# Both tables made straight from x1, three of them kept in DRAM, first batches last in their slot, and e1 spread by TensorE

## What is computed

```python
def _L0_gnn_ref(V, adj, w1, w2, w3, bias):
    o1 = jnp.matmul((adj == 1).astype(jnp.float32), jnp.matmul(V, w1))
    o2 = jnp.matmul((adj == 2).astype(jnp.float32), jnp.matmul(V, w2))
    o3 = jnp.matmul((adj == 3).astype(jnp.float32), jnp.matmul(V, w3))
    return o1 + o2 + o3 + bias

def _L1_gnn_ref(X, adj, W, b, we1, be1, we2, be2):
    h = X @ W.T + b
    e1 = h @ we1 + be1
    e2 = h @ we2 + be2
    e = e1 + e2.T
    e = jnp.where(e >= 0, e, LEAKY_SLOPE * e)
    scores = jnp.where(adj > 0, e, NEG_INF)
    attention = jax.nn.softmax(scores, axis=1)
    return attention @ h
x = _layernorm(x + _L0_gnn_ref(x, adj, ...), axis=-1)
x = _layernorm(x + _L1_gnn_ref(x, adj, ...), axis=-1)
```

## Time and profile before

| | |
|---|---|
| three runs, median (lowest to highest) | 1557.63 us (1556.46 to 1559.41) |
| the profiled execution: its time | 1559.72 us |
| the profiled execution: its span | 1558.1 us |
| TensorE matmul busy | 1422.6 us, 91% |
| VectorE busy | 1092.0 us, 70% |
| ScalarE busy | 978.1 us, 63% |
| GpSimd busy | 116.1 us, 7% |

### The profile page before, as it was taken

How to read it: one execution, slowest core, us unless ns; L and a number is a source line. 1 busy time by engine, 2 the same in 40 slices (tenths; PEclk the granted TensorE clock), 3 DMA queues, 4 the chain that set the end, 5 groups by cost and what they waited for, 6 DMA issues and landing times. The chain is left out here.

```text
span 1558.1 us, 19404 instructions
## 1 busy us (share of the span) xinstructions
PE 1422.6 (91%) x6934; PEld 670.4 (43%) x6934; DVE 1092.0 (70%) x2432; ACT 978.1 (63%) x1534; POOL 116.1 (7%) x154
## 2 busy tenths in 40 slices
PE   0867697989999999999999987999999999999996
PEld 0433243444444444444444433444444444444443
DVE  3677667877877868768778657576667676666663
ACT  1333526457457556456456559787888788788873
POOL 2111011100110100100100021000000000000000
PEclk9999799999999999999999997999999999999998
DMA  9999999993979979967969311000000000100100
GB/s 133 138 126 116 126 110 119 128 114 49 117 96 99 106 69 123 83 68 96 84 67 119 28 62 47 8 28 28 28 28 28 28 28 28 55 28 28 35 1 15
DMA packets 87684, 109.60 MB, mean 70 GB/s; under 512 B 4960, under 2 KB 71072, under 8 KB 87584
## 3 DMA queue, kind: packets, MB, share of 16 engines
q0 software_dynamic: 67584, 67.12, 47.1%
q1 hardware_dynamic: 20000, 41.20, 8.0%
HBM read 296.49 MB, written 13.14 MB: 199 GB/s over the span
## 5 line engine op out<-in xcount | busy, mean ns | idle before, releaser
L1222 PE MATMUL ps<-pos_masks,tables 128*128 128x512 fp8e4 x2048 | 616.4, 383 | 39.2 <-DVE pos_masks L607 32.1
L1004 ACT ACTIVATE neg_masks<-e_row,cols 128x512 int8<-128x512 f32 x816 | 509.7, 708 | 110.9 <-PE ps L1222 46.3
L1222 PE MATMUL ps<-neg_masks,tables 128*128 128x512 fp8e4 x1632 | 492.1, 383 | 0.0
L1180 PE MATMUL ps<-edge_masks,tables 128*128 128x512 fp8e4 (+1 forms) x2048 | 464.1, 385 | 0.0
L1222 PEld LDWEIGHTS ps<-pos_masks,tables 128*128 128x128 f16 x2048 | 200.4, 99 | 285.9 <-issue 49.5
L1180 PEld LDWEIGHTS ps<-edge_masks,tables 128*128 128x128 f16 x2048 | 201.4, 99 | 233.3 <-issue 13.7
L1222 PEld LDWEIGHTS ps<-neg_masks,tables 128*128 128x128 f16 x1632 | 161.3, 99 | 197.7 <-issue 9.0
L605 DVE TENSOR_TENSOR neg_masks<-pos_masks,neg_masks 128x2048 uint16<-128x2048 uint16 x102 | 125.0, 1225 | 91.4 <-ACT neg_masks L1004 88.3
L589 DVE TENSOR_SCALAR edge_masks<-edges 128x512 uint16<-128x512 uint16 x512 | 123.4, 306 | 78.1 <-PE ps L1180 78.1
L589 DVE TENSOR_SCALAR pos_masks<-edges 128x512 uint16<-128x512 uint16 x512 | 114.2, 285 | 88.4 <-PE ps L1222 88.4
L992 ACT ACTIVATE edges<-ps 128x1024 uint8<-128x1024 bf16 x64 | 65.1, 1017 | 172.5 <-PE ps L1189 172.5
(11 more groups left out here) (133 smaller groups left out, 845.0 us busy)
## 6 DMA issues: line engine op xcount, KB each, us to landing
adj_in<-adj POOLq DMA_DIRECT2D x84, 512.0 KB, 12.2
tables<-adj POOLq DMA_DIRECT2D x28, 512.0 KB, 31.2
e_row<-e_scratch SPq DMA_DIRECT2D x34, 256.0 KB, 3.9
edges<-adj POOLq DMA_DIRECT2D x16, 512.0 KB, 11.9
part_scratch<-a_c_rows SPq DMA_DIRECT2D x18, 256.0 KB, 2.5
part_in<-part_scratch SPq DMA_DIRECT2D x18, 256.0 KB, 3.0
edges<-x SPq DMA_DIRECT2D x8, 512.0 KB, 6.6
x_rows<-x SPq DMA_DIRECT2D x8, 512.0 KB, 5.5
```

Of the source, the lines that this page charges most:

```text
L1004: ins = e.activation(gate_bufs[GATE[m]][:, n:n + GR].bitcast(I8), e1row[:, q % 2, :], ACT.Sign, bias=t2[:, JC * c + j:JC * c + j + 1])
L1180: ins = e.matmul(ps[:, h, :], v_hl[:, i, JC * c + j, :], U0[:, n:n + GR].bitcast(kind), start=c == 0 and j == 0 and i == 0, stop=c == NCH ...
L1222: ins = e.matmul(z_bank(q, k), tab[:, c, 2 * k + i, j, :], mask[:, n:n + GR].bitcast(F8A), start=first and j == 0 and i == 0, stop=final a ...
```

## The change

**Tables.** `high` now multiplies x1 by the row factor and rounds in one instruction per tile of 127 columns (8 for each of b and d), and one small instruction writes the factor itself in the last column. `low` does the same on VectorE: 8 `scalar_tensor_tensor` of 127 columns and one of 8, for each of b and d. `table_products`, `ones_column`, the read of x1 and GpSimd's products are gone. This is done in the tail of every block, 4 to 6 too; their tables are formed in yT and xg, and SyncE stores them to DRAM (`tab_dram`, 2 stores of 512 KB for each block) and reads them back after layer 0 (6 loads of 512 KB, ahead of `row_of(LOWS)` in its list). ScalarE's high stands at off 4, for S = 0 and 1 ahead of convert, for the others behind it. VectorE's low stands at the end of slot off 4 for S = 0 and of off 5 for the others. In SyncE's list the read of the next block's x no longer waits for the tables of blocks 0 to 3.

**Order of the late segments.** Groups 2 and 3 come ahead of groups 0 and 1, so that the first two late batches (slots 69 and 70) use tables 2 and 3.

**Fresh batches.** On VectorE masks(m) of a fresh batch stands behind edge_masks(k-1, 1), on TensorE batch(m) behind turn(k).

**First row of e1.** For the fresh segment of each block TensorE spreads e1 to all partitions with 4 f32 matmuls of 128 columns between the two halves of layer0(k-2) in slot off 4 (`e1_spread`), and ScalarE copies it to e1row ahead of the gates. SyncE's 7 row DMAs for these segments are gone.

**Last block.** For S = 7 both halves of o_of follow one another on TensorE, into two banks, and both v_of stand behind the masks of their slot.

The diff, cut to its core:

```diff
+LATE = [2, 3, 0, 1] + list(range(4, 2 * NS))
...
-    for g in range(2 * NS):
+    for g in LATE:
         segs.append((g, [c for c in range(NS) if c not in seen.get(g, ())]))
...
+FRESH = [sum(len(EARLY[b]) for b in range(S)) for S in range(NS - 1)]
-AGAIN = (K, K + 1, K + 2)
+STAGED = (4, 5, 6)
...
+def fresh(m):
+    return SLOTS[m] == NCH * (BATCH[m][1] // 2 + 1) + START
...
             def next_rows(S):
                 e.wait_ge(s_er, S + 1)
-                ge(e, s_lo, min(S + 1, 4))
+                if S in STAGED:
+                    for n in range(2):
+                        e.wait_ge(s_lo, S + 1)
+                        e.dma_start(tab_dram[S - 4, n], (yT, xg)[n][:, :, :].rearrange("p a b -> p (a b)"))\
+                            .then_inc(s_tabst, 16)
+                    e.wait_ge(s_tabst, 16 * (2 * (S - 3)))
                 xg_load(S + 1)
...
+            def table_load(S):
+                e.wait_ge(s_l0, 2 * K)
+                e.wait_ge(s_tabst, 16 * 2 * (S - 3))
+                for n in range(2):
+                    e.dma_start(tab[:, S, 2 * n:2 * n + 2].rearrange("p k j d -> p (k j d)").bitcast(F32),
+                                tab_dram[S - 4, n]).then_inc(s_tabin[S - 4], 16)
...
                 for n in range(len(EARLY[S])):
-                    row_of(q)
                     if n == 0:
                         next_rows(S)
+                    else:
+                        row_of(q)
...
-            for n in range(3):
-                x1_again(n)
+            for S in STAGED:
+                table_load(S)
             row_of(LOWS)
...
-            def low(S, pb, pd):
-                for k, src in ((0, pb), (2, pd)):
+            def low(S):
+                for k, f in ((0, bq), (2, dq)):
+                    hi, lo = table_place(S, k), table_place(S, k + 1)
                     e.wait_ge(s_hi, 2 * S + k // 2 + 1)
-                    ins = e.tensor_tensor(tab[:, S, k + 1], src, tab[:, S, k], ALU.subtract)
+                    for t in range(RB):
+                        j = JC * S + t
+                        e.scalar_tensor_tensor(lo[:, t, 0:D - 1], X1[:, t, 0:D - 1], f[:, j:j + 1],
+                                               hi[:, t, 0:D - 1], ALU.mult, ALU.subtract)
+                    ins = e.tensor_tensor(lo[:, :, D - 1], f[:, JC * S:JC * (S + 1)], hi[:, :, D - 1], ALU.subtract)
                 ins.then_inc(s_lo, 1)
...
                 for S, off in tails(k):
-                    if off == 2:
+                    if off == 2 and S < NS - 1:
                         v_of(S, 0)
                 for m in at(k):
-                    masks(m)
-                    after(m)
+                    if not fresh(m):
+                        masks(m)
+                        after(m)
...
                 if 1 <= k <= K:
                     edge_masks(k - 1, 1)
+                for m in at(k):
+                    if fresh(m):
+                        masks(m)
+                        after(m)
...
+                    if off == 4 + min(S, 1):
+                        low(S)
...
+            def e1_spread(S):
+                q = FRESH[S]
+                ge(e, s_gate, 0 if q < 2 else END[q - 2] + 1)
+                ge(e, s_min, q - 1)
+                e.wait_ge(s_e1sp, S + 1)
+                e.activation(e1row[:, q % 2, :], ps[:, 3, :], ACT.Copy).then_inc(s_row[q % 2], 16)
...
+            def high(S):
+                if S in (2, 3):
+                    e.wait_ge(s_pk, GUEST[S] + 1)
+                e.wait_ge(s_x1, S + 1)
+                e.wait_ge(s_er, S + 1)
+                e.wait_ge(s_bd, 2 * (S + 1))
+                for k, f in ((0, bq), (2, dq)):
+                    hi = table_place(S, k)
+                    for t in range(RB):
+                        j = JC * S + t
+                        e.activation(hi[:, t, 0:D - 1], X1[:, t, 0:D - 1], ACT.Copy, scale=f[:, j:j + 1])
+                    e.activation(hi[:, :, D - 1], f[:, JC * S:JC * (S + 1)], ACT.Copy).then_inc(s_hi, 1)
...
+            def e1_spread(S):
+                e.wait_ge(s_e1Tc, S + 1)
+                for t in range(GT):
+                    ins = e.matmul(ps[:, 3, t * P:(t + 1) * P], idf[0:RB, t:t + 1].broadcast_to([RB, P]), e1T[:, :],
+                                   start=True, stop=True)
+                ins.then_inc(s_e1sp, 1)
...
                 for m in at(k):
-                    batch(m)
-                    after(m)
+                    if not fresh(m):
+                        batch(m)
+                        after(m)
                 if k < K:
                     turn(k)
+                for m in at(k):
+                    if fresh(m):
+                        batch(m)
+                        after(m)
```

131 lines of the change are left out of this document (52 added, 79 removed).

## The result

The change makes the kernel slower. Its median is 1580.43 us (1578.66 to 1583.61, 4 runs) against 1558.52 us for the kernel before (1556.46 to 1560.19, 4 runs beside them): a ratio of 1.0143, 95% interval 1.0122 to 1.0165. The forecast was 1572, with a range of 1556 to 1586. The profiled execution of the changed kernel is 20.2 us longer than that of before, though TensorE has only 12.5 us more busy time.

The account below looks back on a forecast made before the run. TensorE was taken as the bound, busy 1422.6 of 1558.1 us. Terms 17.6 + 5.0 + 4.7 + 1.5 - 6.5 - 7.2 = 15.1, less 1 for slots 26 and 34, gave 1557.6 + 14 = 1572 us, range 1556 to 1586.

Parts of the forecast that it names:

- Blocks 4 to 6: In each, TensorE waits 4.1 us around the turn, plus 0.9 of spread and some slow clock; 17.6 us lost in sum.
- The turn splits the new one in two, so I take half of it: At fresh batches, a pause can cost 1.7 us more by slow clock; half taken because the turn divides the new pause.
- Block 3: Same walk as block 4, less 0.6 us already idle and masks 0.2 sooner: 4.2 to 5.9 us lost, middle 5.0.
- Block 2: turn(29) ahead of batch 8 brings 7 us of waiting behind layer0(27); 3.8 to 5.5 us lost, middle 4.7.
- block 1: By block 2's steps, batch 2 starts at 272.6 and layer0(20) at 279.5 to 281.2; 0.7 to 2.4 us lost, middle 1.5.
- Block 0: The row comes some 10 us earlier as the x load no longer waits; gain 5 to 8 us, middle 6.5.
- After layer 0: Block 7's new order and earlier tables bring batch 49 forward; gain 7.2 us, range 4 to 10.
- VectorE's new load at nothing: On VectorE, low(S), some 4.6 us, is covered by batch 24 and layer0(44), 13.8 us of TensorE, so it costs nothing.
- the fresh masks stay hidden: Rival: edge_masks(k-1, 1) doesn't hold the masks, so blocks 3 to 6 cost only the spread, 3.6 us; 1553 us, chance 0.10.
- 1545 us case: Rival: fresh masks stay hidden and the stretch after layer 0 loses all its 15 us idle; chance 0.04.
- Worse: Rival: ScalarE later, six pauses each 1 to 2 us longer and slow, nothing won after layer 0; 1588 us, chance 0.09.
- even case: Rival: lateness holds, but all 15 us idle after layer 0 go and waits of slots 18 to 26 shrink; 1559 us, chance 0.13.

Follow-up runs that it names:

- r4: The changed kernel, late order kept, without the spread: all rows of e1 come by DMA ahead of the next x load; 1578.75 us, 1.0131 to the kernel before.
- r1: The changed kernel with fresh batches put back: masks ahead of the packing on VectorE, batch ahead of the turn on TensorE; 1552.71 us, 0.9947.
- v4: r1 with the spread only in blocks 0 to 2, and block 7's o_of(7, 1) and v_of(7, 0) back in their old order; 1554.94 us, 0.9969.
- v7: v6 with block 7's tables split one slot later on ScalarE and VectorE, and its row sums a slot after that; 1533.82 us, 0.9840.
- v8: v7 with the row sums of blocks 0 to 6 one slot later on VectorE, behind the second batch's masks; 1524.09 us, 0.9778.
- v3: r1 with the spread only in blocks 0 to 2, and convert ahead of an early segment's first gates unless its batch is fresh; 1549.70 us, 0.9937.
- v6: v3 with the row of segment q+1 issued ahead of the store of segment q-1's sums in SyncE's list; 1541.61 us, 0.9905.

## Why the prediction was right, and where its terms were off

The side, the mechanism and the range were right. The forecast of 1572 us lies 8.4 below the median. The ledger's 21.4 against 14.1 gives the terms of the miss.

- **Blocks 4 to 6: 21.1 in place of 17.6.** The waits came as forecast: 3.86 us against 4.1, split 1.97 and 1.89 around the turn where 2.5 and 1.5 stood in the forecast, with pos_masks behind an edge_masks released by layer0. Two sizes were off. The spread takes 1.15 us (the first row of the other places) and moves layer0 by 1.2, not 0.9. And the clock, of which I took half (0.85), was paid in full: 8.59 - 6.91 = 1.68 us in block 4, the same for batches 16 and 32, and 1.6 for batch 40. "The turn splits the new one in two, so I take half of it" is the step that failed: the turn of 0.6 us between the two waits saved nothing. The rule of the Trainium skill that was weighed there ("TensorE: Matmul & The Clock Gate", HAM oscillation) made the sum 5 us higher, and the trace agrees with it at these pauses. The last 0.3 us are the two overlaps of 0.16 that a pause between two instructions takes away.
- **Block 3: 6.3 in place of 5.0.** The same two sizes.
- **Block 2: 5.0 (forecast 4.7), block 1: 4.7 (forecast 1.5).** turn(29) waited 7.21 and turn(21) 5.82 us for packed_bf, against 6 to 7. Block 1 has 1.5 us from a slow layer0(17) behind a wait of 2.38 us that the kernel before has too, with no slowness behind it, then 1.5 in slot 20 and 1.7 from the pause. The forecast had the spread and the pause, but not the slow layer0(17), and not that high(1) ahead of convert(20) holds turn(20): r4 has no spread, yet TensorE waits 1.36 us there. The clock was also mis-sized: turn(21) and batch 2 took 0.83 + 9.21 us, 2.7 more than at full speed, where 0 to 1.7 stood in the forecast.
- **Block 0: -7.8 in place of -6.5.** turn(14) stands at 198.56, forecast 199.5; the masks of batch 0 end at 176.3, forecast 175.8. Right in mechanism. What wasn't seen is that the late order costs 6.8 us here too: r1 gains 14.6.
- **After layer 0: -7.1 in place of -7.2.** Batch 49 at 989.89 is 22.2 us later than in the earlier trace rows, where TensorE was 29.6 later at the end of layer 0, so it stands 7.4 earlier against that end. The walk's steps came too: against the end of layer 0, batch 46 starts within 0.3 us of its forecast place and batch 49 within 0.9. v4 and v7 confirm the reasons: the order of block 7, the tables made early, and low(7) with the row sums still ahead of masks(49).
- **Slots 26 and 34: nothing recovered**, forecast 1. **The rest, to batch 127: -1.1**, within the 3 us that the prediction allowed.
- **VectorE's new load at nothing** was right under the late order, where its cover of a batch and a layer0 exists. v8 shows that it isn't right when the order is undone.

Of the rivals, "the fresh masks stay hidden" fell by the trace: edge_masks is released by layer0 at 632.07. The 1545 us case fell with it. "Worse" had its full clock in blocks 3 to 6, but not its loss after layer 0. The even case needed all idle time after layer 0 to go, and v7 shows the kind of edit that this would have taken.

## What to carry to other kernels

Before an instruction is moved behind another on an in-order engine, ask what that other one waits for: here a ready batch of 6.9 us was put behind a turn, and its masks behind an edge_masks whose buffer comes free only when layer0 ends, and so the batch stopped being the cover for both. Follow a pause to the head of its chain, for moving convert only moved the wait to the next instruction (v3), while issuing the row 15 us sooner removed most of it (v6). A change that loses can hold parts that win: undoing one order turned +1.4% into -0.5%, and the further moves up to v8 made that -2.2%.
